# Graph kernel, counting stage: all digit casts on ScalarE, and two instead of three one-hot tiles per block there

## The reference

```python
deg = maximum(segment_sum(ones(E), dst), 1);  norm = deg ** -0.5
h = x
for _ in range(10):
    agg = segment_sum((h * norm)[src], dst)
    h = agg * norm * 0.9 + x * 0.1
x = layernorm(x + h)
```

## Time and profile before

| what | value |
|---|---|
| median of three runs | 3280.54 us |
| the profiled execution, its own time | 3281.08 us |
| its span | 3279.3 us |
| granted TensorE clock over the span | 0.794 |
| busy over the span | TensorE 64%, VectorE 65%, ScalarE 38%, GpSimd 55% |
| busy in the counting stage (80 to 312 us) | TensorE 172 us, VectorE 210 us, ScalarE 183 us, GpSimd 79 us of 232 |

### The profile page before, as it was taken

How to read it: one execution, slowest core, us unless ns; L and a number is a source line. 1 busy time by engine, 2 the same in 40 slices (tenths; PEclk the granted TensorE clock), 3 DMA queues, 4 the chain that set the end, 5 groups by cost and what they waited for, 6 DMA issues and landing times.

```text
span 3279.3 us, 42810 instructions
## 1 busy us (share of the span) xinstructions
PE 2113.7 (64%) x14281; PEld 1829.1 (56%) x14282; DVE 2144.2 (65%) x5719; ACT 1254.9 (38%) x1357; POOL 1794.8 (55%) x1772
## 2 busy tenths in 40 slices
PE   2875999999999556666546766743333344555455
PEld 1553999999999444444434555533333334455444
DVE  7997766677668476666647777764444445555565
ACT  1886676666767333333233333410000003222222
POOL 3333222222222477777477777737777767777771
PEclk7997999999999777777767778876666665667667
DMA  2100000000000545544254555532333224444441
GB/s 65 25 1 1 0 0 0 0 0 0 0 0 0 166 129 140 141 140 136 78 155 136 158 159 160 155 91 72 84 85 98 59 56 127 132 134 135 135 119 38
DMA packets 151135, 271.50 MB, mean 83 GB/s; under 512 B 33642, under 2 KB 95702, under 8 KB 150918
## 3 DMA queue, kind: packets, MB, share of 16 engines
q0 software_dynamic: 71152, 185.67, 20.8%
q1 hardware_dynamic: 43142, 60.09, 5.9%
q10 hardware_dynamic: 36692, 23.93, 2.4%
HBM read 241.94 MB, written 27.85 MB: 82 GB/s over the span
## 4 chain that ended last, share of the span: by engine, by line
POOL 38%; issue 13%; DVE 7%; PE 7%; DMA 2%; ACT 1%; ACTq 0%; POOLq 0%; DVEq 0%
POOL t_rows L2231 17%; POOL t_rows L2648 10%; POOL t_rows L2981 10%; PE t_sum_ps L2339 2%; DVE t_rows L2431 1%; PE t_sum_ps L2669 1%; DVE t_onehot L2158 1%; DMA t_rows<-rel_table_b,t_rel 1%; DMA t_rows<-gat_table,t_src 1%; PE t_small_ps L2309 0%; DMA t_rows<-kv_table_b,t_src 0%; PE t_product_ps L1960 0%; PE t_small_ps L2834 0%; PE t_product_ps L2842 0%; DVE t_stage L3065 0%
## 5 line engine op out<-in xcount | busy, mean ns | idle before, releaser
L2231 POOL DMA_INDIRECT t_rows<-gat_table,t_src x794 | 759.5, 957 | 302.3 <-issue 239.1
L1256 PE MATMUL hop_ps<-parts,wide 128*128 128x256 f32 x5900 | 712.5, 283 | 4.8 <-DVE parts L1352 3.6
L1256 PEld LDWEIGHTS hop_ps<-parts,wide 128*128 128x128 f32 x5900 | 709.7, 192 | 6.8 <-issue 3.4
L1307 ACT CAST wide<-counts 128x3200 fp32r<-128x3200 fp8e4 x177 | 506.2, 2863 | 231.5 <-PE hop_ps L1256 211.2
L2339 PE MATMUL t_sum_ps<-t_rows,t_onehot 128*128 128x264 f32 x1660 | 468.2, 450 | 101.9 <-DVE t_rows L2431 101.9
L1317 POOL CAST wide<-counts 128x3200 fp32r<-128x3200 fp8e4 x59 | 168.7, 2859 | 581.3 <-PE hop_ps L1256 564.4
L2339 PEld LDWEIGHTS t_sum_ps<-t_rows,t_onehot 128*128 128x128 f32 x1660 | 371.5, 227 | 182.2 <-issue 105.0
L2648 POOL DMA_INDIRECT t_rows<-rel_table_b,t_rel x397 | 379.0, 955 | 170.4 <-issue 168.5
L2981 POOL DMA_INDIRECT t_rows<-kv_table_b,t_src x397 | 378.6, 954 | 135.1 <-issue 119.1
L2669 PE MATMUL t_sum_ps<-t_rows,t_onehot 128*128 128x128 f32 x830 | 148.6, 362 | 288.1 <-DMA t_rows<-rel_table_b,t_rel 288.1
L2669 PEld LDWEIGHTS t_sum_ps<-t_rows,t_onehot 128*128 128x128 f32 x830 | 144.4, 275 | 297.1 <-issue 295.5
(11 more groups left out here) (447 smaller groups left out, 3297.3 us busy)
## 6 DMA issues: line engine op xcount, KB each, us to landing
t_dst_wide<-dst_row SPq DMA_DIRECT2D x72, 544.0 KB, 4.1
rel_table_b<-t_stage ACTq DMA_DIRECT2D x25, 512.0 KB, 3.6
t_rows<-gat_table,t_src POOLq DMA_INDIRECT x794
t_rows<-rel_table_b SPq DMA_DIRECT2D x18, 512.0 KB, 3.8
t_rows<-rel_table_b,t_rel POOLq DMA_INDIRECT x397, 2.5
t_rows<-kv_table_b,t_src POOLq DMA_INDIRECT x397, 2.8
gat_table<-t_own ACTq DMA_DIRECT2D x10, 520.0 KB, 3.9
kv_table_b<-t_fresh ACTq DMA_DIRECT2D x5, 512.0 KB, 5.1
```

The costliest lines, as they stand in the source:

```text
L1256: last = nc.tensor.matmul(ps[bank][0:columns.shape[-1], 0:2 * D], columns[:, k, :], parts[old][:, k, :], start=(k == 0), stop=(k == NB - 1))
L1307: nc.scalar.copy(wide[b % B][:, :, :], column(b)).then_inc(widened, 1)
L2231: c.nc.gpsimd.indirect_dma_start(t.rows[:, slot(k), 0:FW], None, self.table, bass.IndirectOffsetOnAxis(ap=t.src[:, k:k + 1], axis=0)).then ...
```

## The change

Three edits, all in `count_edges`. GpSimd's two digit casts and their wait are gone. `unpack` on ScalarE does all five digits. `BY_ACT` names the tiles 4 and 15 instead of 3, 9 and 15, so that a whole block has 15 VectorE tiles instead of 14, and ScalarE's second tile now comes behind `unpack`. The last block has one ScalarE tile, as before (4 in place of 3).

```diff
-BY_ACT = (3, 9, 15)
+BY_ACT = (4, 15)
...
                         nc.gpsimd.memset(x[:, NB - 1, :], 0.0).then_inc(x_zeroed, 1)
-                    pool.wait_ge(digits, 2 * b + 2)
-                    nc.gpsimd.tensor_copy(target(b, 3), digit(b, 3), saturate=False).then_inc(unpacked, 1)
-                    nc.gpsimd.tensor_copy(target(b, 4), digit(b, 4), saturate=False).then_inc(unpacked, 1)
...
                 def unpack(b):
                     act.wait_ge(digits, 2 * b + 2)
-                    for f in (0, 1, 2):
+                    for f in range(FIELDS):
                         nc.scalar.copy(target(b, f), digit(b, f), saturate=False).then_inc(unpacked, 1)
                 for b in range(NB):
                     mine = [k for k in tiles_of(b) if k in act_at]
                     column_hot(mine[0])
                     if b:
                         to_int(b - 1)
-                    if len(mine) > 1:
-                        column_hot(mine[1])
                     if b:
                         unpack(b - 1)
-                    if len(mine) > 2:
-                        column_hot(mine[2])
+                    for k in mine[1:]:
+                        column_hot(k)
```

## The result

| kernel | median of 14 runs | lowest to highest |
|---|---|---|
| before | 3281.94 us | 3278.14 to 3284.93 |
| changed | 3289.87 us | 3284.54 to 3291.63 |

The ratio is 1.0021, with a 95% interval of 1.0014 to 1.0029. So the change costs 7.9 us, slower by a little more than 0.2%. The forecast was +11.1 us.

What follows compares the result with a forecast made beforehand. VectorE was taken to bound the counting stage, busy 210 of 232 us. Interval, copy and tail terms gave +7.8 and the lower clock +3.3, together +11.1, for a median of 3291.5 us; range 3280 to 3300.

Steps and rivals of the forecast that it cites:

- The mechanism: Ordinary blocks of the counting stage: late tile 15 delays TensorE, VectorE waits for the ring; loop 8.4 us; chance 0.57.
- VectorE is all that counts: Counting stage would end when VectorE's list does: -10 us, 3271; chance 0.11.
- Only ScalarE's loop counts: Ordinary loop would be ScalarE's 8.16 us, TensorE passing its tiles meanwhile: 3284, no change; chance 0.20.
- The lower clock in all blocks: Pause ahead of tile 15 lowers TensorE's clock in fifteen blocks: 16 us in place of 3.3, 3304; chance 0.12.
- rest: Remaining terms in the 3284 rival's sum, beside ordinary intervals and degree copies; given as -0.2 us.
- fifteen ordinary intervals: Intervals between splits go from 8.07 to 8.40 us: 4.95, less 1.4 for ring waits already contained: +3.5.
- the lower clock: TensorE's lower clock level on tiles 15, 16, 0 and 1: 1.1 us a block, three blocks, +3.3.
- four degree copies: Where VectorE waits for degree matmuls (L1150), the copy starts 6.49 us after the split, before 5.39: +4.1.
- two intervals with `own_edges`: VectorE, late there anyway, loses its hold-up and makes tile 9 itself: -0.3 us each, -0.6.
- first `locate`, and L1185 with L1186: Two intervals whose extra VectorE work fits in its slack of 0.7 us; both become 8.4: -0.1 together.
- block 0: One more VectorE tile ahead of the first split: +0.4 us.
- the tail: Block 24: `to_int` behind five casts, then five casts on ScalarE ending at 300.4, GpSimd's ended at 299.84: +0.5 us.

Runs made afterwards that it cites:

- e3: Changed kernel with ScalarE tiles 4 and 9 instead of 4 and 15, tile 9 before the five casts; 3268.3 us, 0.9962 of before.
- e7: Changed kernel with one tile (4) on ScalarE instead of two, VectorE making tile 15 too; 3279.4 us, 0.9996 of before.
- e1: Kernel before with all five digit casts on ScalarE, none on GpSimd, tiles 3, 9 and 15 kept; 3302.5 us, 1.0066 of before.
- e4: Changed kernel with a ring of eight slots instead of six for hot_column; 3280.7 us, 0.9999 of before.
- e2: Kernel before with tiles 4 and 15 on ScalarE, the second behind the casts, GpSimd keeping its two casts; 3291.6 us, 1.0032 of before.

## Why the prediction was right, and where it was off

**The mechanism** was the forecast's: slower, by a new ring wait behind a late tile 15. The loop was given as 8.4 and measured as 8.41. In the block shown above, counted from the split's end at 215.77, each step came within 0.05 us of its forecast: the tile at 4.03 (4.08), its first matmul at 5.09 (5.14), the degree matmuls at 5.67 (5.69), tile 0 at 6.30 (6.32), VectorE's tile 6 at 6.81 (6.83), the split's end at 8.42 (8.44). The degree copy was to start 6.49 after the split's end and started at 6.47. The wait of TensorE for tile 15 (over 1 us) and ScalarE's wait of about a split's length (1.24) are there. VectorE's ring waits come to 10.1 us where near 12 were named, and its tiles to 439 ns on average where 440 were. e3 and e7 show that it is this mechanism: both take tile 15 away from behind the casts, with the same or more work for the bound engine, and gain 21.6 and 10.5 us.

**The rivals.** *VectorE is all that counts* fell with e1, which freed VectorE and lost 20.6 us. *Only ScalarE's loop counts* gives the right number for a kernel with eight slots; with six it isn't enough, as e4 shows. (The steps written in the prediction end at 7.24 + 0.89 = 8.13, which is what e4 measured; its 8.16 holds 0.03 that no step names.) *The lower clock in all blocks* fell with the profile after: twelve of fifteen ordinary intervals took 8.40 to 8.42. Two figures beside these are slips that change nothing: the "rest" in the second rival's sum is +0.2 by the prediction's own terms, not -0.2, and 3280.54 + 11.1 is 3291.6.

**The sum** in detail, from the starts of the splits in the two profiled executions:

| term of the sum | predicted, us | measured, us |
|---|---|---|
| fifteen ordinary intervals | +3.5 | +4.0 without, +4.8 with the clock's part |
| the lower clock | +3.3 | +0.8 (in the line above) |
| four degree copies | +4.1 | +4.5 |
| two intervals with `own_edges` | -0.6 | -1.7 |
| first `locate`, and L1185 with L1186 | -0.1 | +0.2 |
| block 0 | +0.4 | -0.2 |
| the tail | +0.5 | +0.5 |

The stage as a whole grew by 8.05 us (ScalarE's first copy of the hops starts at 319.89, before at 311.84), and the stages behind it took 1.2 us less in this execution, which gives the 6.8 of the spans. Without the clock the terms were to give +7.8 and gave +7.3, and that closeness is in part luck: two intervals with `own_edges` and block 0 came out 1.7 us lower than reckoned, the ordinary ones, the degree copies and the two smaller places 1.2 us higher. The term that was mis-sized is the lower clock. I had multiplied 1.1 us with three blocks. Eight ordinary intervals met the lower level for some of their time, not three, but only three of them paid, and at most 0.43 us: the number of blocks was not too high, but the price was. Ordinary intervals of the changed kernel (from split to split; PE busy, PEld, DVE, ACT, POOL, then PEclk, DMA share, GB/s):

```profile
106.35:114.76 8.41, 7.08 (x63) 5.44 (x62) 7.73 (x20) 7.11 (x10) 0.00 (x0) 0.87 0.07 10
114.76:123.45 8.69, 6.55 (x59) 4.44 (x58) 7.88 (x20) 7.10 (x10) 0.00 (x0) 0.93 0.81 169
123.45:131.87 8.42, 7.09 (x63) 5.42 (x62) 7.75 (x21) 7.10 (x10) 0.00 (x0) 0.87 0.12 34
159.36:168.20 8.84, 6.70 (x59) 4.47 (x58) 7.81 (x20) 7.10 (x10) 0.00 (x0) 0.91 0.01 2
269.87:278.27 8.40, 7.07 (x63) 5.60 (x62) 7.73 (x20) 7.10 (x10) 0.00 (x0) 0.85 0.01 2
```

The three with the lowest clock (0.85 to 0.87) take 8.40 to 8.42, no more than a block at the full one. There the lower level fell on tiles that TensorE makes while it would soon have to wait for ScalarE's tile 15 in any case, and the pause of 1.3 us took it up. The two shown that were longer had a higher mean, with the lower level at their end. Tile 0 of the next block comes 7.2 us after an interval's start. In the three longer ordinary intervals the lower level began 7.2, 7.4 and 7.6 us after it and cost 0.43, 0.28 and 0.10 us; where it began at 7.7 it cost nothing. So the price follows how much of the tiles 0 and 1 it covered. (It isn't the DMA traffic of the 8.69 one, a share of 0.81: the 8.84 one has 0.01.) The price of 1.1 was reckoned for a lower clock on the tiles 15, 16, 0 and 1 together, and no block showed it; I took the worst place for every one. The Trainium skill ("TensorE: Matmul & The Clock Gate", What's actually happening) says that the throttled level is the default and that activity lifts it, which let one fear much more of the lower level here. The trace agrees in direction: with longer pauses eight ordinary intervals met the lower level, where three had, and the stage's mean went down a little, from 0.88 to 0.86 over windows of 232 and 240 us, in part because the second holds more of the stage's tail; over 89 to 293 us it is 0.92 and 0.91. Hardly any time hung on it.

The intervals with `own_edges` gained more than reckoned, 0.6 and 1.2 in place of 0.3 each. The freed VectorE accounts for 0.3; the rest wasn't taken apart. In the second of them TensorE was at the lower level for 6.8 us in the kernel before and for 4.5 in the changed one, which may be a part of it. Why block 0 got no longer wasn't followed up either.

## What to carry to other kernels

When work moves to another engine, don't add up busy times: write down the loop of the engine that receives it, in the order of its list, and see which result the in-order consumer needs that now stands behind the moved work. A result that others wait for belongs ahead of bulk work that nobody waits for yet, and an engine that must wait for a step elsewhere should have an independent piece to do meanwhile; here that was worth 21.6 us without one instruction more or less. And a buffer ring turns a late piece into a stall as soon as its depth is less than the lateness: two slots more took 9 us off the same order.

## What the runs showed of the hardware that I had not expected

What the lower TensorE clock costs depends on the tiles that it falls on, and not on how low a block's mean is. In the changed kernel it was free where TensorE waits anyway: 0.85 over a block without a tenth of a microsecond lost. Where it fell on tiles whose ring slots another engine was waiting for, a block got longer by 0.10 to 0.43 us in the changed kernel, by 0.6 to 0.7 in e2, and by 0.1 to 1.1 in e1. In the kernel before it is the same: three ordinary intervals met the lower level, and they took 8.50, 8.50 and 8.66 us, while the other twelve took 7.99 to 8.11. With a ring of eight (e4) it cost an ordinary interval nothing. No run held the clock fixed: this is read from which blocks met the lower level and which didn't.

A GpSimd cast held up two VectorE tiles a block by 0.40 us each, and still removing all of it gained nothing in e1, where ScalarE set the pace. It showed only once the order was right: e3 has a block of 7.56 us against 8.07, with a tile more on VectorE.

GpSimd's indirect DMA instructions took longer than before, 1093 ns against 980 on average. They are now issued six in a row instead of in pairs; that this is the reason isn't shown (groups of the counting stage):

```profile
L961 POOL DMA_INDIRECT own_rows<-edges_in_order,cnt_last_at x25 | 27.3, 1093 | 180.2 <-DVE cnt_last_at L1151 174.1 <-issue 6.1
```

The prediction's sum has 0 for them, and that holds: VectorE waits 1.9 us in all for fetched rows, as before.
